# Attention with a ternary feed-forward layer on one core: a new order of the opening, products of ones at the start, and denominator constants kept as a column

## What is computed

```
q = feature_map(split(x @ Wq.T + bq), orf)      # 16 heads of 32, 128 features:
k = feature_map(split(x @ Wk.T + bk), orf)      # (exp(proj - norm) + 1e-6) / sqrt(128)
v = split(x @ Wv.T + bv)
kv, ksum = einsum('nlm,nld->nmd', k, v), sum(k, axis=1)
out = q @ [kv, ksum];  out = out[..., :-1] / out[..., -1:]
x = layernorm(x + out @ Wo.T + bo)
scale = max(mean(|W|), 1e-5);  w3 = clip(round(W / scale), -1, 1)
x = layernorm(x + x @ (w3 * scale).T)
```

## Time and profile before

| | |
|---|---|
| device time, median of 3 runs | 1328.44 us (1326.99 to 1329.98) |
| the profiled execution's own time | 1326.88 us, of which span 1325.0 us |
| granted TensorE clock, mean | 0.993 |
| PE busy | 1277.0 us, 96% of the span |
| PEld, DVE, ACT, POOL busy | 961.2, 969.8, 696.8, 513.3 us |

### The profile page before, as it was taken

How to read it: one execution, slowest core, us unless ns; L and a number is a source line. 1 busy time by engine, 2 the same in 40 slices (tenths; PEclk the granted TensorE clock), 3 DMA queues, 4 the chain that set the end, 5 groups by cost and what they waited for, 6 DMA issues and landing times.

```text
span 1325.0 us, 24976 instructions
## 1 busy us (share of the span) xinstructions
PE 1277.0 (96%) x8522; PEld 961.2 (73%) x8522; DVE 969.8 (73%) x1821; ACT 696.8 (53%) x1337; POOL 513.3 (39%) x1005
## 2 busy tenths in 40 slices
PE   6999999999999999999999999999999999999796
PEld 5766788677877678776787668876688667886565
DVE  5688865887668875788658787578865787658875
ACT  5466535574355743557336653466544664455543
POOL 1234443254333453335424344334443344432433
PEclk9999999999999999999999999999999999999998
DMA  6567404674146721467115761267503674046511
GB/s 210 136 150 191 125 32 109 167 183 101 52 106 163 198 65 57 124 156 195 60 57 128 193 166 48 69 147 203 140 32 87 169 193 102 32 118 144 134 49 47
DMA packets 94013, 160.34 MB, mean 121 GB/s; under 512 B 31168, under 2 KB 47680, under 8 KB 93376
## 3 DMA queue, kind: packets, MB, share of 16 engines
q1 hardware_dynamic: 67712, 139.51, 40.9%
q10 hardware_dynamic: 9792, 17.12, 3.5%
q0 software_dynamic: 16384, 2.13, 1.1%
HBM read 39.13 MB, written 16.78 MB: 42 GB/s over the span
## 4 chain that ended last, share of the span: by engine, by line
PE 82%; DVE 7%; ACT 3%; issue 3%; SPq 3%; DMA 2%; POOL 1%; ACTq 0%; DVEq 0%; POOLq 0%
PE ps L835 29%; PE ps L872 23%; PE ps L933 7%; PE ps L858 4%; PE ps L904 4%; PE ps L860 4%; PE ps L859 4%; PE ps L891 3%; PE ps L949 2%; DMA rows<-in_x_t 1%; ACT features L602 1%; SPq L453 1%; SPq L442 1%; DVE squares_turned L753 1%; DVE stacks L715 1%
## 5 line engine op out<-in xcount | busy, mean ns | idle before, releaser
L602 ACT ACTIVATE features<-ps 128x512 f32<-128x512 f32 x512 | 278.8, 601 | 271.4 <-PE ps L835 200.0
L508 POOL DMA_DIRECT2D stacks<-norm_rows x512 | 253.0, 502 | 413.1 <-DVE norm_rows L768 172.6
L835 PE MATMUL ps<-Wo_hi,stacks 128*128 128x512 f32 x512 | 171.6, 401 | 4.5 <-DVE stacks L715 4.1
L487 POOL TENSOR_SCALAR stats<-stats 128x1 f32<-128x1 f32 x128 | 37.0, 289 | 328.3 <-DVE stats L697 328.3
L710 DVE TENSOR_TENSOR den<-den,features 128x512 f32<-128x512 f32 x192 | 134.7, 701 | 13.5
L576 ACT ACTIVATE values_then_attention<-ps 128x512 f32<-128x512 f32 x64 | 38.3, 599 | 199.0 <-PE ps L860 196.4
L835 PE MATMUL ps<-W_ternary,stacks 128*128 128x512 f32 x512 | 129.7, 396 | 6.2 <-DVE stacks L818 6.2
L933 PE MATMUL ps<-features,kv_ksum 128*32 128x512 f32 x1024 | 123.1, 598 | 10.0 <-ACT features L602 7.1
L835 PE MATMUL ps<-orf_key_a,stacks 128*128 128x256 f32 x512 | 131.7, 288 | 0.7 <-DMA stacks<-norm_rows 0.7
L835 PE MATMUL ps<-orf_key_b,stacks 68*128 68x256 f32 x512 | 128.5, 283 | 0.0
L551 ACT ACTIVATE rows<-rows,stats 128x512 f32<-128x512 f32 x128 | 101.0, 812 | 44.1 <-POOL stats L491 43.0
(11 more groups left out here) (112 smaller groups left out, 2649.3 us busy)
## 6 DMA issues: line engine op xcount, KB each, us to landing
stacks<-unit_hi SPq DMA_DIRECT2D x384, 128.0 KB, 2.4
stacks<-unit_lo SPq DMA_DIRECT2D x256, 128.0 KB, 3.2
stacks<-unit_hi SPq DMA_DIRECT2D x64, 256.0 KB, 3.8
out<-rows ACTq DMA_DIRECT2D x64, 256.0 KB, 2.0
rows<-in_x_t SPq DMA_DIRECT2D x56, 256.0 KB, 3.5
stacks<-norm_rows POOLq DMA_DIRECT2D x512, 4.0 KB, 2.6
rows<-in_x SPq DMA_DIRECT2D x32, 256.0 KB, 3.7
features<-in_x SPq DMA_DIRECT2D x32, 256.0 KB, 4.4
```

Of the source, the lines that this page charges most:

```text
L508: pool.dma_start(slot[row:row + 1, c:c + L].rearrange("o (t c) -> o t c", c=DH), NN[DH * h:DH * (h + 1), u % 2, part, :].bitcast(F32)).the ...
L602: nc.scalar.activation(FE[:, n % 8, :, 0:M], ps[:, :].rearrange("p (a m) -> p a m", a=HG), ACT.Exp, scale=C_EXP).then_inc(a_exp.sem, 1)
L835: last = mm(out, a, b, start=(n == 0), stop=(n == len(terms) - 1))
```

## The change

- The products of ones: PE first waits for POOL's `ones` and then does 24 products of `ones` with `ones` (128x128, float32) into bank DN, whose content nobody reads.
- The opening: SP loads chunk 0 of Wv, then tile 0 of x, then the rest of Wv. The load of the output bias goes from ACT's queue to SP's, behind all tiles of x. ACT and DVE split Wv 0 and 1, tile 0 of x, then Wv 2 and 3. `constant_rows` (C 1) comes right behind C 0, ahead of the first projection; the split of Wq moves from before V 3 to between and behind the halves of the first projection; Q and N of unit 0 go behind V 4. P waits for two chunks of its weight at a time.
- The ternary chunks (WF), four at the end of unit 2 of batch 0, are done at the end of units 1, 2 and 3 and once inside unit 3. The first four loads of x for batch 1 go from unit 2 to the end of unit 3 with them.
- The denominators: `turned` is a new tile `dens_turned` of 16 blocks of 34 columns. Column 32 of each block holds the constant, written by ACT in step KVT (as is `CC`), and DVE sums columns 31 and 32 instead of adding a scalar to column 0.

```diff
-        if u == 2 and b == 0:
-            seq += [("WF", 0, k) for k in range(KT)]
-        if u == 2 and b + 1 < B:
+            seq += [("WF", 0, 1)]
+        if u == 2 and 0 < b < B - 1:
             seq += [("LX", b + 1, t) for t in range(4)]
...
+        if u == 1 and b == 0:
+            seq += [("WF", 0, 0)]
+        if u == 3 and b == 0:
+            seq.insert(seq.index(("L", 0, 5, 0)) + 1, ("WF", 0, 2))
+            seq += [("WF", 0, 3)] + [("LX", 1, t) for t in range(4)]
...
-PROLOGUE = first("W", 0) + first("LW", 1) + first("XT", 0, 1, 2, 3) + first("V", 0) + first("W", 1) + first("LW", 2)
-PROLOGUE += first("XT", 4) + first("V", 1) + first("XT", 5, 6, 7) + first("V", 2) + [("C", 0, 0)] + first("W", 2) + first("V", 3)
-PROLOGUE += projected(0, 0) + projected(0, 1) + [("N", 0, 0), ("LIFT", 0, 0), ("NL", 0, 0), ("C", 0, 1)] + first("V", 4)
+PROLOGUE = [("W", 0, 0, 0), ("W", 0, 0, 1)] + first("XT", 0) + [("W", 0, 0, 2), ("W", 0, 0, 3)] + first("LW", 1)
+PROLOGUE += first("XT", 1, 2, 3) + first("V", 0) + first("W", 1) + first("LW", 2)
+PROLOGUE += first("XT", 4) + first("V", 1) + first("XT", 5, 6, 7) + first("V", 2) + [("C", 0, 0), ("C", 0, 1)] + first("V", 3)
+PROLOGUE += projected(0, 0)[:4] + [("W", 0, 2, 0), ("W", 0, 2, 1)] + projected(0, 1)[:4] + [("W", 0, 2, 2), ("W", 0, 2, 3)]
+PROLOGUE += first("V", 4) + [("Q", 0, 0, 0), ("Q", 0, 0, 1), ("N", 0, 0), ("LIFT", 0, 0), ("NL", 0, 0)]
...
                 sp.dma_start(raw["v"][:, k, :], by_chunk(wv)[:, k, :]).then_inc(s_wv[k], 16)
-            for t in range(4):
+                if k == 0:
+                    load_x(0, 0)
+            for t in range(1, 4):
                 load_x(0, t)
...
+            sp.dma_start(BO[:, :], bo.unsqueeze(0).broadcast_to([P, D])).then_inc(s_bld, 16)
...
+                elif kind == "KVT":
+                    act.wait_ge(a_kc.sem, a_kc.nth(b, 3 * u + 3))
+                    act.wait_ge(v_dr.sem, v_dr.nth(b, 4 * u))
+                    nc.scalar.activation(turned[:, :, DH], RSUM[:, 2 * u + 1:2 * u + 2].broadcast_to([P, 16]), ACT.Copy,
+                                         scale=EPS).then_inc(a_c.sem, 1)
+                    nc.scalar.activation(CC[:, 2 * u:2 * u + 1], RSUM[:, 2 * u:2 * u + 1], ACT.Copy, scale=EPS).then_inc(a_c.sem, 1)
...
-                elif kind == "G" and at[1] == 7:
-                    dve.wait_ge(a_kc.sem, a_kc.nth(b, 3 * u + 3))
-                    nc.vector.tensor_scalar(CC[:, 2 * u:2 * u + 2], RSUM[:, 2 * u:2 * u + 2], EPS, None,
-                                            ALU.mult).then_inc(v_c.sem, 1)
...
-                    nc.vector.transpose(turned, DN[:, :]).then_inc(v_dt.sem, 1)
+                    nc.vector.transpose(turned[:, :, 0:DH], DN[:, :].rearrange("p (a c) -> p a c", c=DH)).then_inc(v_dt.sem, 1)
                     dve.wait_ge(v_dt.sem, v_dt.nth(b, 2 * g + h + 1))
-                    dve.wait_ge(v_c.sem, v_c.nth(b, g + 1))
-                    nc.vector.tensor_scalar(den, turned.rearrange("p (a c) -> p a c", c=DH)[:, :, 0], CC[:, 2 * g + 1:2 * g + 2],
-                                            None, ALU.add).then_inc(v_dr.sem, 1)
+                    dve.wait_ge(a_c.sem, a_c.nth(b, 2 * g + 2))
+                    nc.vector.reduce_sum(den, turned[:, :, DH - 1:DH + 1], axis=mybir.AxisListType.X).then_inc(v_dr.sem, 1)
...
+            pe.wait_ge(s_ones, 1)
+            for _ in range(WARM):
+                mm(DN[:, 0:P], ones[:, :], ones[:, :], start=True, stop=True)
...
-                    if b == 0 and u < 2 and h == 0 and part == 0:
-                        pe.wait_ge(s_wlo, 8 + 4 * u)
+                    if b == 0 and u < 2 and h == 0:
+                        pe.wait_ge(s_wlo, 6 + 4 * u + 2 * part)
```

More of the change, by code:

```diff
@@ L55 @@
 QK = 3 * DH + 2
+WARM = 24
 KK = 2 * DH + 4
@@ L115, in unit_stages @@
             seq += [("LR", b, t) for t in range(4)]
-        return seq + [("R", b, g, 1)]
+        seq += [("R", b, g, 1)]
+        if u == 1 and b == 0:
[3 more added lines that the diff above has]
+            seq += [("WF", 0, 3)] + [("LX", 1, t) for t in range(4)]
+        return seq
     v0 = [("V", b + 1, 0)] if two else []
@@ L229, in attention_kernel @@
         DR = sb("den", [P, 2, HALF])
+        DT = sb("dens_turned", [P, 16 * (DH + 2)])
         cols = sb("cols", [P, 128])
@@ L239, in attention_kernel @@
         RSUM, CC, WSUM = col(28, 2 * NG), col(36, 2 * NG), col(44, KT)
+        turned = DT[:, :].rearrange("p (a c) -> p a c", c=DH + 2)
         by_token = [col(64 + 16 * h, 16) for h in range(2)]
@@ L271, in attention_kernel @@
         a_exp, a_kc = Signal("features_ready", 8 * NU), Signal("kv_copied", 3 * NG)
+        a_c = Signal("eps_sums_ready", 2 * NG)
         a_ahi = Signal("a_hi_ready", TT)
@@ L277, in attention_kernel @@
         v_ks = Signal("features_added", 7 * NG)
-        v_kvc, v_c = Signal("kv_ready", NG), Signal("eps_sums_ready", NG)
+        v_kvc = Signal("kv_ready", NG)
         v_dt, v_dr = Signal("den_turned", 2 * NG, 1), Signal("den_steps", 2 * 2 * NG)
@@ L315, in attention_kernel @@
             "setup_bias_product", "setup_bias", "setup_w_abs", "setup_w_sum", "setup_w_scale", "setup_ternary"))
-        s_pin = sem("carries_a_wait")
+        s_pin, s_bld, s_ones = sem("carries_a_wait"), sem("setup_bo_loaded"), sem("setup_ones_written")
         s_wv = [sem(f"setup_wv{k}") for k in range(KT)]
@@ L464, in fill_where @@
                                         pattern=pattern, channel_multiplier=cm).then_inc(s_k, 1)
+            nc.gpsimd.memset(ones[:, :], 1.0).then_inc(s_ones, 1)
             nc.gpsimd.memset(ident[:, :], 0.0)
-            nc.gpsimd.memset(ones[:, :], 1.0)
             nc.gpsimd.memset(KVS[:, 0:2, :], 0.0)
@@ L537, in _ @@
             act.dma_start(orf_t, orf).then_inc(s_ld, 16)
-            act.dma_start(BO[:, :], bo.unsqueeze(0).broadcast_to([P, D])).then_inc(s_ld, 16)
             def split_hi(b, t):
@@ L558, in _ @@
                         act.wait_ge(s_w[u - 1], 16)
-                    for k in range(KT):
+                    for k in at[1:] or range(KT):
                         if u == 0:
@@ L645, in constant_columns @@
                 dve.wait_ge(s_k, 5)
-                dve.wait_ge(s_ld, 16 * 4)
+                dve.wait_ge(s_ld, 16 * 3)
                 nc.vector.tensor_scalar(ABC, BC, A_SQ, None, ALU.mult)
@@ L729, in _ @@
                     dve.wait_ge(s_bvo, 1)
+                    dve.wait_ge(s_bld, 16)
                     nc.vector.tensor_tensor(BO[:, :], DN[:, :], BO[:, :], ALU.add).then_inc(s_bo, 1)
@@ L773, in _ @@
                     add_features(b, u // 2, at[1])
-                elif kind == "G" and at[1] == 7:
-                    dve.wait_ge(a_kc.sem, a_kc.nth(b, 3 * u + 3))
-                    nc.vector.tensor_scalar(CC[:, 2 * u:2 * u + 2], RSUM[:, 2 * u:2 * u + 2], EPS, None,
-                                            ALU.mult).then_inc(v_c.sem, 1)
                 elif kind == "GG":
                     g, h = u, at[1]
-                    n, turned, den = 2 * (2 * g + h), DR[:, h, :], by_token[h]
+                    n, den = 2 * (2 * g + h), by_token[h]
                     dve.wait_ge(t_gg.sem, t_gg.nth(b, 2 * g + h + 1))
                     dve.wait_ge(v_a.sem, v_a.nth(b, 2 * g + h - 1))
-                    nc.vector.transpose(turned, DN[:, :]).then_inc(v_dt.sem, 1)
+                    nc.vector.transpose(turned[:, :, 0:DH], DN[:, :].rearrange("p (a c) -> p a c", c=DH)).then_inc(v_dt.sem, 1)
                     dve.wait_ge(v_dt.sem, v_dt.nth(b, 2 * g + h + 1))
-                    dve.wait_ge(v_c.sem, v_c.nth(b, g + 1))
-                    nc.vector.tensor_scalar(den, turned.rearrange("p (a c) -> p a c", c=DH)[:, :, 0], CC[:, 2 * g + 1:2 * g + 2],
-                                            None, ALU.add).then_inc(v_dr.sem, 1)
+                    dve.wait_ge(a_c.sem, a_c.nth(b, 2 * g + 2))
+                    nc.vector.reduce_sum(den, turned[:, :, DH - 1:DH + 1], axis=mybir.AxisListType.X).then_inc(v_dr.sem, 1)
                     dve.wait_ge(v_dr.sem, v_dr.nth(b, n + 1))
```

## The result

The changed kernel takes 1315.40 us, median of 4 runs (1314.52 to 1316.20); in the same session the kernel before took 1327.72 us, median of 4 (1326.20 to 1329.98). The ratio is 0.9892 with a 95% interval of 0.9867 to 0.9916: 1.1% faster (the two medians alone give 0.9907). The profiled execution took 1315.64 us, its span is 1313.8 us. The prediction was 1317.0 with a range of 1313.5 to 1321.5.

The account below looks back on a forecast made before the run. PE, busy 1277.0 of 1325.0 us, was taken as the bound. Terms -6.5 - 1.0 - 4.1 + 0.7 = -10.9 us on 1326.88 gave 1316.0, raised to 1317 for the median; range 1313.5 to 1321.5.

Parts of the forecast that it names:

- the opening: From kernel start to unit 0's features: they start at 47.9 us, not 54.4; term -6.5 us.
- its three terms: Behind the first features: ternary chunks -1.0 us, denominators -4.1 us, ACT's extra writes +0.7 us.
- three signs of being wrong: Ones ending behind 10 us, a wait over 1 us before V 4, or waits for ACT's features above 9 us.
- from the profiled execution to the median: Whole kernel: half of the 1.56 us by which the median before exceeds its profiled execution is added, 1316.0 to 1317.
- ACT: Two small ACTIVATEs more in each of 32 KVT steps, 0.35 us for both, lengthen PE's waits for features: +0.7 us.
- First product: Opening: 24 products of ones take 7.5 us, and V 0 starts at 8.6 us at the high clock.
- Loads and `constant_rows`: Opening: loads land 1.0 us earlier, Wk at 12.6; `constant_rows` ends at 24.5; 0.4 us wait before V 4.
- What the ones are worth: Opening, before V 0: 2.1 us of idle time and 2.4 us of slow clock saved.
- Ternary: Batch 0, chunks moved from the end of unit 2: PE no longer waits for `kv_ksum`; -1.0 us.
- Denominators: Unit 7: a TENSOR_REDUCE isn't held by POOL's work as a TENSOR_SCALAR is, ending PE's L715 waits; -4.1 us.
- the rival of the slow transpose: Denominators: the transpose with gaps is taken piece by piece, 2.6 us more each, time 1340; chance 0.05.
- whoever comes second is blocked: Skill's rule cited for the denominators: `tensor_scalar` can take the port pair VectorE shares with GpSimd; the later one waits.

Follow-up runs that it names:

- the six of the table: Changed kernel, and it with old denominators, POOL's additions twice, ternary chunks back, ACT's writes doubled, or ones in the last batch: features start at 47.18 to 48.58 us.

## Why the prediction was right or wrong

The direction and the main mechanisms were right, and the sum was near: -11.2 us of PE's work against -10.9, 1315.64 us for the profiled execution against 1316.0. That it is so near is in part luck: the opening gave 0.7 us less than its term and the stretch 1.0 more than the -4.4 of its three terms. None of the three signs of being wrong came. What failed are two terms, the first of them the step from the sum to the forecast.

- **The step that failed: from the profiled execution to the median.** "Part of such a spread may be batches in which DVE met POOL, which the change ends. I take half of it" raised 1316.0 to 1317. Measured, the median of the changed kernel lies 0.2 us below its profiled execution, so this term was 0.8 us (1.0 with the rounding) of the 1.6 us by which the forecast missed. By the ratio of 0.9892 the gain is 14 us, more than the 11.2 of the traces, so the step went the wrong way. Its reason fails too: the spread doesn't go with the denominators. The four kernels with `constant_rows` at its old place and the long wait for `unit_lo` (POOL's work undoubled) spread by 8 to 11 us (before 8.2 in 16 runs, new denominators alone 9.5 in 11, ones alone 10.7 in 12, `constant_rows` back 8.6 in 9), those with the new opening by 1.3 to 4.9 (4 to 6 runs each, which by itself narrows them), the one with old denominators among them (3.9). The standard deviations, which don't grow with the number of runs, are 2.2 to 2.8 us and 0.6 to 2.0. What an unprofiled execution did isn't known; the profiles show only that behind that wait the clock had fallen in two of these four kernels and not in the two others, 1.5 and 2.3 us apart.
- **ACT, the term of the sum that failed.** The writes cost 0.46 us a group, above the 0.35 assumed. The prediction let them meet PE as longer waits for features, with ACT's waits for x taking up part: +0.7. (By its own rule, 0.35 us less the waits of 0.8, 0.2, 0.3, 0, 0.6, 0 and 1.4, that sum is 0.9.) The waits for features didn't grow (7.1 us before and in the kernel with the new denominators alone, 5.5 in the changed kernel). PE met the writes at the split of x instead, 0.2 us in each of seven batches, 1.4 us in all: twice the size, and a place that the prediction didn't name.
- **First product.** Right. V starts at 8.39 (predicted 8.6), its products 0.2265 us apart; the ones take 7.26 us (7.5). It is no fixed number: in six executions with these ones V started at 8.17 to 9.45, as the clock rose earlier or later in them. (In the kernel before it rose at 15.5 us, not 15.1: products are 0.427 us apart up to there.)
- **Loads and `constant_rows`.** Right within the spread of executions. In the profiled execution Wk landed at 13.25 us, 0.4 earlier than before and not 1.0; from there the chain ran as worked out (5.4 us of `constant_rows`, ending 25.08), the wait ahead of V 4 was 0.92 us and not 0.4, and the features started at 48.58, not 47.9. But in the ten executions with the new order of loads Wk landed at 11.89 to 13.25, the middle 12.3, and in the four with the old one at 13.26 to 13.77; and in the six of the table the features started at 47.18 to 48.58, the middle 48.1. So the term of -6.5 stands, and the -5.8 of the ledger are a late execution. The wait ahead of V 4 came where V started early (8.2 to 8.4) and Wk landed late (13.0 to 13.3).
- **What the ones are worth.** The prediction's 2.4 us of slow clock are there (2.2 to 2.4 without the ones). Its 2.1 us of idle time before the first product are not the work of the ones: without them V starts at 8.17. Nor do the parts of the opening add up one by one: `constant_rows` moved is worth 6.8 us or more in the new order, the ones 0.9 to 2.3, and ones alone, or ones and loads without that move, nothing.
- **Ternary.** Right in the trace: the wait of 1.2 us is gone and is 1.1 us when the chunks are put back (predicted 1.0).
- **Denominators.** Right: of the 4.1 us of waits for the split 0.2 are left. -4.1 was predicted, -3.4 with ACT's writes, which come and go with it; measured are 3.8 us in the stretch when both are taken out of the change, 2.8 when added alone, and by the ratios 4.2 (0.9924 - 0.9892, times 1328) and 5.0 us, of which only the last is clear of the intervals. The reduce takes 0.198 us and never over 0.205, the transpose with gaps its 717 ns, which ends the rival of the slow transpose.

What stays open is the rest of that spread, and how much of the opening's gain in the median is the clock. Why the waits for features are 1.6 us shorter than before is open too.

## What to carry to other kernels

An instruction of 0.24 us may hold an engine for microseconds while another engine works (here VectorE while GpSimd added): look at the most, not the mean, of such a group, and change its kind before you move it. Where several things delay the start, find the chain that ends last before pricing any of them; here nothing was gained without one move, and the products that raise the clock were worth something only once nothing stood between them and the work. Before naming the term that was off, look at the same code in the traces of the other kernels: a difference of 0.7 us in one execution of the opening was within what it does by itself. Price a filler from a row of that very form (records, not calls), and end it short of the event it waits for.

## What the runs showed of the hardware

- A wait of about 2 us for PE may or may not cost the high clock: behind 2.20 us at 39.92 the kernel before went on with products 0.23 us apart, behind 2.21 us at 39.38 the kernel with ones alone with 0.427. The length of a wait doesn't tell which. Waits of 2.20 and 2.21 us at that place kept it in two more kernels (12 products in 2.85 us).
- By the recorded starts, an addition that comes first can still be held: six that started 0.77 to 0.87 us ahead of the first of POOL's additions of the bias were, and others at 0.86 to 0.94 weren't. Ahead of POOL's splits of x, additions that started only 0.37 us before went free. The prediction's "whoever comes second is blocked" can't be read off POOL's recorded starts, which are rough.
- A float32 product of 128x128 by 128x128 is two records and 0.229 us at the high clock (84 records in 9.62 us); at the low clock a record takes 0.213 us.
- A 32x32 block transpose of 128x512 that writes its blocks 34 columns apart takes 717 ns, as without a gap.
- Two kernels with the same code behind output stage 7 differ by up to 2.8 us there (47.84 to 50.64 us among all kernels), and the granted clock differs with it: 0.94 over this part in the kernel before (50.62 us), 1.00 in that with ScalarE's writes doubled (47.84 us). A statement on the whole time of a single execution can't be finer than that.
